# Operands of VectorE in the bring stage of a graph network kernel: SBUF against PSUM

## Chip, cores, metric

One NeuronCore of a Trainium2 chip runs the whole program. The metric is the time of one execution on the device in microseconds (us), median over the runs shown.

## What is computed

Two graph layers over 6250 nodes and 206250 edges (100000 random pairs in both directions and a loop for each node, sorted by destination), each after a layer norm with ReLU and each added to its input:

```
h = max(layernorm(x), 0)
x = x + edge_layer(h)        # per edge: silu(silu([h[src], h[dst], attr, weight/5] @ ew1 + eb1) @ ew2 + eb2)
                             # summed over the edges of a row, then a node MLP, residual
h = max(layernorm(x), 0)
x = x + gat(h)               # two attention layers: 4 heads x 32 with ReLU, then 1 head x 64
```

The edge layer sums by source node, while the edges arrive sorted by destination. So the kernel first brings each edge's part of the hidden layer to its place in an order by source. That is the bring stage, the one that the change is in.

## The kernel before

Edges are cut into chunks of 128 that belong to one tile of 128 destination nodes; four chunks (U = 4) are a group, and the bring stage has 415 groups (SUPER). Each engine runs its own program. `edge_pipeline` writes out the first 8 groups, runs the rest in a loop of 8 groups a round and then the tail; a step of an engine handles a group some steps behind the newest. All order between engines is by counting semaphores that the code waits on; on one engine the order is that of the code.

In the bring stage, for a group:
- SP loads four records of 128 edges (L471) and two columns of places (L473), ScalarE's queue the other two columns (L756).
- VectorE (`bring`, L1309 to L1346) works out the slots: small instructions on 128x4 at L1324, L1327, L1328, L1329, L1337, L1341 and L1343, and one long one at L1334, which compares the row of lane numbers 0..127 (`lanes`) with each edge's lane and so writes a one-hot matrix of 128x512 in bf16. L1341 writes into the buffer `z_out` and waits first (L1339) until the puts of the group eight earlier, which used that buffer, have landed.
- TensorE turns the one-hots and the records (L950, L952), two steps later it multiplies (L935, L938) into banks 2 and 3 of PSUM. It uses banks 0 to 5 in this stage. ScalarE copies out of PSUM (L745, L746, L738).
- GpSimd (`put`, L633 to L642) waits for ScalarE's copy and for VectorE's slots and issues four indirect DMAs at L640, called puts here: each writes 128 rows of 132 numbers to the places in `z_s`, in DRAM, that a column of slots in SBUF names.

Where an edge goes in the order by source is worked out by `rank` (L1231 to L1245), once for each of 49 tiles and each of four parts of the edges (310, 434, 434 and 434 columns). It is five VectorE instructions, each of which waits for the one before: L1237 compares the keys with the tile number into `found`; L1239 is a running sum over `found` (the scan's second operand is a zero, broadcast) into `counted`; L1241 saves its last column; L1243 multiplies the compare with the running sum; L1245 adds that to the places. Part 0 is ranked ahead of the stage (L1251). Parts 1 to 3 are ranked inside it: groups 8 to 151 each carry one `rank` step behind their own instructions (L1344), and at three cuts one more step and the conversion L1249 follow (`next_part`). Then the remaining 263 groups have none.

Behind it come the edge stage (`edge_mlp`), which sums into banks 6 and 7, the node stage and the two attention layers, in which GpSimd gathers rows with an indirect DMA at L690 and VectorE reduces PSUM (L1490, L1486), multiplies (L1576) and adds into sums (L1588 with SBUF operands, L1593 with one operand in PSUM).

All PSUM is one tensor `ps_all`; `ps[n]` is its bank n, 512 fp32 columns wide.

Of the kernel before, what the change touches and what calls it, by code (L numbers as in the profile page):

```python
# [15 lines left out]
ALU = mybir.AluOpType  # L16
# [3 lines left out]
P = 128  # L20
# [7 lines left out]
U = 4  # L28
# [9 lines left out]
PARTS = (310, 434, 434, 434)  # L38
# [106 lines left out]
def part_cols(k):  # L145

    return slice(PART_AT[k], PART_AT[k] + PARTS[k])
# [27 lines left out]
def gnn_kernel(nc, x, ids_in, src_in, dst_next, rec_in, ew1, eb1, ew2, eb2, nw1, nb1, nw2, nb2,  # L175
               W1, a_src1, a_dst1, b1, W2, a_src2, a_dst2, b2, out):
    ctx = ExitStack()
    with ctx:
        def sb(name, shape, dt=F32):
            return ctx.enter_context(nc.sbuf_tensor(name, shape, dt))[tuple(slice(None) for _ in shape)]  # L180

        def sem(name):
            return ctx.enter_context(nc.semaphore(name))
# [28 lines left out]
        lanes = sb("lanes", [P, P])  # L212
# [4 lines left out]
        signs_at = sb("signs_at", [P, NB + 1])  # L217

        picks = [sb(f"pick{n}", [CODE + 3 * h, h, P], BF16) for n, (h, _) in enumerate(LAYERS)]
        lower = sb("lower", [P, P])  # L220
        ones = sb("ones", [P, P])
        ones_b = sb("ones_b", [P, P], BF16)
        zero = sb("zero", [P, 1])
# [52 lines left out]
        def carve(start, shape, dt=F32):  # L276
            words = 1
            for n in shape:
                words *= n
            words = words if dt != BF16 else words // 2  # L280
            v = arena[:, start:start + words]
            assert start + words <= ARENA, (start, shape)
            if dt != F32:
                v = v.bitcast(dt)
            names = " ".join("abcd"[:len(shape)])
            kw = {"abcd"[n]: shape[n] for n in range(len(shape))}
            return v.rearrange(f"p ({names}) -> p {names}", **kw), start + words
# [23 lines left out]
        src_hit, src_scan = (acc[:, 2 * COLS + k * max(PARTS):2 * COLS + (k + 1) * max(PARTS)] for k in range(2))  # L311
# [6 lines left out]
        dst_hot, at = carve(at, [4, U, P], BF16)  # L318
# [49 lines left out]
        ps = [ps_all[:, 512 * n:512 * (n + 1)] for n in range(8)]  # L368
# [3 lines left out]
        def S(name):  # L372
            if name not in s:
                s[name] = sem(name)
            return s[name]

        block = ctx.enter_context(nc.Block())

        class Rounds:
# [5 lines left out]
            def load(self, i):  # L385
                _, self.values = nc.values_load_multi_w_load_instructions(
                    self.table[0:1, bass.ds(i - self.back, self.count)], engines=(self.engine,), min_val=0, max_val=self.top,
                    skip_runtime_bounds_check_because="counts of comparisons, and starts that a minimum bounds")

            def of(self, g):  # L390
                if g.i is None:
                    return self.eng.value_load(self.table[0:1, bass.ds(g.at, 1)], min_val=0, max_val=self.top)
                return self.values[g.off + self.back]

        def four(engine, table, g, top):
            _, values = nc.values_load_multi_w_load_instructions(
                table[0:1, bass.ds(g.at * U, U)], engines=(engine,), min_val=0, max_val=top,
                skip_runtime_bounds_check_because="counts of comparisons, and starts that a minimum bounds")
            return values

        @block.sync
        def _(sp):
            sp.dma_start(xs, x.rearrange("(t p) f -> p t f", p=P)).then_inc(S("x_in"), 16)

            for to, ends, name in ((dst_i, ids_in[1:2, :].rearrange("a n -> (a n)"), "dst_in"), (next_i, dst_next, "next_in"), (src_i, src_in, "src_in")):
                for k in range(len(PARTS)):
                    sp.dma_start(to[:, part_cols(k)], edges_of(ends, k).rearrange("(p j) -> p j", p=P)).then_inc(S(name), 16)
            sp.wait_ge(S("weights_clear"), 2)
            loads = [
                (w_src, ew1[0:F_IN, :]), (w_dst, ew1[F_IN:2 * F_IN, :]),  # L410
# [713 lines left out]
        def _(dve):  # L1124
            link = Chain(dve, S("dve_step"))
# [105 lines left out]
            def rank(k, tile, ran):  # L1231

                small = S("rank_step")
                no, come = lanes[:, bass.ds(tile, 1)], carry[:, bass.ds(tile, 1)]
                keys, places = key[:, part_cols(k)], place[:, part_cols(k)]
                found, counted = src_hit[:, 0:PARTS[k]], src_scan[:, 0:PARTS[k]]
                dve.tensor_scalar(found, keys, no, None, ALU.is_equal).then_inc(small, 1)  # L1237
                dve.wait_ge(small, ran + 1)
                dve.tensor_tensor_scan(counted, found, zero.broadcast_to([P, PARTS[k]]), come, ALU.add, ALU.add).then_inc(small, 1)  # L1239
                dve.wait_ge(small, ran + 2)  # L1240
                dve.tensor_scalar(come, src_scan[:, PARTS[k] - 1:PARTS[k]], 1.0, None, ALU.mult).then_inc(small, 1)  # L1241
                dve.wait_ge(small, ran + 3)
                dve.scalar_tensor_tensor(counted, keys, no, counted, ALU.is_equal, ALU.mult).then_inc(small, 1)  # L1243
                dve.wait_ge(small, ran + 4)
                dve.tensor_tensor(places, places, counted, ALU.add).then_inc(small, 1)  # L1245
# [5 lines left out]
            with dve.Fori(0, NT) as b:  # L1251
                rank(0, b, b * RANK_STEPS)
# [49 lines left out]
            link(dve.tensor_copy(b_part[:, 2, :], b_rest))  # L1302
            dve.sem_inc(S("b_part_ready"), 1)


            dve.wait_ge(S("ordered"), 1)
            dve.sem_inc(S("arena_free"), 1)

            def bring(of):  # L1309
                g = of(0)  # L1310
                if g is None:
                    return
                r = g.slot(4)
                small = S("slot_step")

                def after(k):
                    dve.wait_ge(small, g.back(1).done(SLOT_STEPS) + k)

                dve.wait_ge(S(f"rec_in{r}"), g.uses(4, 16 * U))
                src_col = xr[:, r, :, REC - 2:REC - 1].bitcast(I32).rearrange("p u a -> p (u a)")  # L1320
                dst_col = xr[:, r, :, REC - 1:REC].bitcast(I32).rearrange("p u a -> p (u a)")
                if g.back(1).exists():
                    after(0)
                dve.scalar_tensor_tensor(beyond, lane_node[:, bass.ds(g.at * U, U)], lane_rest, dst_col, ALU.add, ALU.is_le  # L1324
                                         ).then_inc(small, 1)
                dve.wait_ge(S(f"slot_in{r}"), g.uses(4, 16 * U))
                dve.tensor_tensor(to_spare, spare[:, g.slot(SLOTS) * U:(g.slot(SLOTS) + 1) * U], slot_in[:, r], ALU.subtract).then_inc(small, 1)  # L1327
                dve.tensor_scalar(lane_i[:, r], src_col, P - 1, None, ALU.bitwise_and).then_inc(small, 1)  # L1328
                dve.scalar_tensor_tensor(dst_lane[:, r], dst_col, lane_col, lane_node[:, bass.ds(g.at * U, U)], ALU.add, ALU.subtract  # L1329
                                         ).then_inc(small, 1)  # L1330
                if g.back(4).exists():
                    dve.wait_ge(S("x_transposed"), g.back(4).done())
                after(4)
                dve.tensor_tensor(dst_hot[:, r], lanes.unsqueeze(1).broadcast_to([P, U, P]),  # L1334
                                  dst_lane[:, r].unsqueeze(2).broadcast_to([P, U, P]), ALU.is_equal).then_inc(S("dst_hot_ready"), 1)
                after(2)
                dve.tensor_tensor(to_spare, to_spare, beyond, ALU.mult).then_inc(small, 1)  # L1337
                if g.back(SLOTS).exists():
                    dve.wait_ge(S(f"z_put{g.slot(SLOTS)}"), g.back(SLOTS).uses(SLOTS, 16 * U))  # L1339
                after(3)  # L1340
                dve.tensor_copy(z_out[:, g.slot(SLOTS), :, F_HID], lane_i[:, r]).then_inc(small, 1)  # L1341
                after(5)
                dve.tensor_tensor(slot[:, g.slot(SLOTS)], to_spare, slot_in[:, r], ALU.add).then_inc(small, 1)  # L1343
                if 0 < ranking[0] < len(PARTS) and g.i is not None:  # L1344
                    first = SLOTS + (ranking[0] - 1) * PART_ROUNDS * SLOTS
                    rank(ranking[0], g.at - first, g.at * RANK_STEPS + (RANK_STEPS * (NT * ranking[0] - first)))  # L1346
# [3 lines left out]
            def next_part():  # L1350
                k = ranking[0]
                if k > 0:
                    rank(k, NT - 1, RANK_STEPS * (NT * (k + 1) - 1))
                    ranked(k)
                ranking[0] += 1
# [303 lines left out]
```

## Time and profile before

| | |
|---|---|
| time of 3 runs | 9367.48, 9372.87 and 9378.12 us, median 9372.87 us |
| profiled execution | 9370.1 us, span of its trace 9368.2 us |
| busy, share of the span | TensorE 77%, GpSimd 68%, VectorE 65%, ScalarE 52% |
| stages, us from the start | set-up and ranking of part 0 to 343; bring stage 343 to 2617; edge stage to about 4360; attention layers from about 4521 and 7000 to the end |
| costliest group | L690, 3616 gathers, 3471.1 us busy |
| second | L640, 1660 puts, 1755.0 us busy, mean 1057 ns |

A busy share is an average over stages that have different limits, so none of these shares says what binds a stage. For that one reads the chain of work that ended last, the busy time by stretch and the order of time within a group. Each time below is from one profiled execution, in us from the start of the span unless marked ns; L640 is line 640 of the kernel.

### The profile page before, as it was taken

How to read it: one execution, taken by the hardware profiler on the slowest of the kernel's cores; microseconds unless marked ns; L12 is line 12 of the kernel's file. 1: busy time of each engine (PE TensorE's matmuls, PEld its weight loads, DVE VectorE, ACT ScalarE, POOL GpSimd, SP SyncE). 2: the span in 40 equal slices, each digit the busy share in tenths (PEclk: the TensorE clock that was granted, in tenths of full speed). 3: DMA queues.
4: the chain of work that ended last, by engine and by line, in shares of the span. 5: the costliest groups of instructions: out<-in, count | busy, mean ns of one | idle time of the engine just before them, and what ended most of it. 6: DMA issues, size and time to landing. Idle time of an engine off the chain costs nothing.

```text
span 9368.2 us, 235997 instructions
## 1 busy us (share of the span) xinstructions
PE 7249.4 (77%) x52596; PEld 5744.2 (61%) x52823; DVE 6071.2 (65%) x27239; ACT 4885.8 (52%) x11854; POOL 6324.9 (68%) x7563
## 2 busy tenths in 40 slices
PE   2466666666689999998699999999966777777776
PEld 2355555555578888887366666666645555555554
DVE  7777732222233343343799999999976777777776
ACT  4122233333334444443467667777736777777775
POOL 0377777777766666663577777777737777777775
PEclk9988888888899999999555555555555555555555
DMA  4122222222222222221222222222241111111114
GB/s 142 43 54 55 54 59 60 59 61 60 60 75 70 70 72 70 71 71 33 54 55 54 55 54 55 54 55 54 55 33 29 28 28 28 28 28 28 28 28 27
DMA packets 990523, 491.42 MB, mean 52 GB/s; under 512 B 830665, under 2 KB 841468, under 8 KB 990140
## 3 DMA queue, kind: packets, MB, share of 16 engines
q0 software_dynamic: 168832, 302.29, 14.8%
q1 hardware_dynamic: 701756, 169.41, 9.8%
q10 hardware_dynamic: 119840, 18.68, 1.2%
q8 instruction: 31, 0.51, 0.0%
q14 instruction: 64, 0.52, 0.0%
HBM read 356.46 MB, written 151.48 MB: 54 GB/s over the span
## 4 chain that ended last, share of the span: by engine, by line
PE 26%; issue 23%; POOL 23%; DVE 17%; DMA 6%; DVEq 2%; ACT 1%; POOLq 1%; SPq 0%; ACTq 0%
POOL z_s L640 18%; DMA arena<-table,arena 5%; POOL arena L690 5%; PE ps_all L965 5%; PE ps_all L975 4%; PE ps_all L992 4%; PE ps_all L1100 3%; PE ps_all L989 3%; DVE shift L1531 2%; DVE arena L1535 2%; DVE arena L1490 2%; PE ps_all L1076 1%; DVE arena L1576 1%; PE ps_all L1001 1%; PE ps_all L977 1%
## 5 line engine op out<-in xcount | busy, mean ns | idle before, releaser
L690 POOL DMA_INDIRECT arena<-table,arena x3616 | 3471.1, 960 | 1500.5 <-issue 984.6
L640 POOL DMA_INDIRECT z_s<-arena x1660 | 1755.0, 1057 | 853.1 <-issue 504.5
L1100 PE MATMUL ps_all<-arena 128*128 128x132 f32 (+1 forms) x7232 | 1809.1, 429 | 1.8 <-DVE acc L1593 1.8
L1100 PEld LDWEIGHTS ps_all<-arena 128*128 128x128 f32 x7232 | 1606.4, 325 | 2.6 <-issue 2.6
L829 ACT ACTIVATE arena<-lanes_b,arena 128x128 bf16<-128x128 bf16 x3616 | 1147.1, 387 | 415.6 <-DVE arena L1464 407.1
L1490 DVE TENSOR_REDUCE arena<-ps_all 128x2 f32<-128x1024 f32 x904 | 1098.2, 1215 | 18.3 <-PE ps_all L1117 18.3
L1117 PE MATMUL ps_all<-arena,pick 28*128 28x512 bf16 (+1 forms) x2260 | 1081.7, 597 | 0.5 <-DVE arena L1490 0.5
L1076 PE MATMUL ps_all<-ident_b,arena 128*128 128x128 bf16 x3616 | 541.0, 303 | 645.1 <-DMA arena<-table,arena 434.0
L745 ACT ACTIVATE arena<-ps_all 18x512 f32<-18x512 f32 x415 | 243.2, 586 | 1381.0 <-PE ps_all L952 1367.2
L1386 DVE TENSOR_TENSOR arena<-lanes,arena 128x512 f32<-128x512 f32 x452 | 322.8, 714 | 973.8 <-PE ps_all L965 973.8
L853 ACT ACTIVATE arena<-ps_all 28x512 bf16<-28x512 bf16 (+1 forms) x904 | 522.6, 578 | 717.2 <-PE ps_all L1076 717.2
L950 PE MATMUL ps_all<-ident_b,arena 128*128 128x128 bf16 x1660 | 188.1, 245 | 822.7 <-DVE arena L1334 821.4
L1076 PEld LDWEIGHTS ps_all<-ident_b,arena 128*128 128x128 bf16 x3616 | 356.3, 136 | 761.3 <-DVE arena L1477 393.9
L1341 DVE CAST arena<-arena 128x4 f32<-128x4 int32 x415 | 72.9, 176 | 1041.3 <-DMA z_s<-arena 1041.2
L1072 PEld LDWEIGHTS ps_all<-ident_b,arena 128*128 128x128 bf16 x3616 | 303.4, 127 | 654.7 <-issue 647.9
L950 PEld LDWEIGHTS ps_all<-ident_b,arena 128*128 128x128 bf16 x1660 | 108.4, 106 | 903.4 <-DVE arena L1334 755.8
L1072 PE MATMUL ps_all<-ident_b,arena 128*128 128x128 bf16 x3616 | 536.9, 302 | 102.6 <-ACT arena L836 102.6
L935 PE MATMUL ps_all<-w_edge,arena 128*128 128x128 f32 x3320 | 604.4, 341 | 10.3 <-issue 9.3
L935 PEld LDWEIGHTS ps_all<-w_edge,arena 128*128 128x128 f32 x3320 | 544.5, 248 | 67.1 <-issue 44.3
L836 ACT ACTIVATE arena<-arena 128x512 bf16<-128x512 bf16 x904 | 568.9, 629 | 30.9 <-ACT arena L829 0.4
L1088 PE MATMUL ps_all<-arena 128*128 128x8 bf16 (+1 forms) x10848 | 447.3, 169 | 162.7 <-DVE arena L1567 156.1
L1088 PEld LDWEIGHTS ps_all<-arena 128*128 128x128 bf16 x10848 | 427.9, 109 | 215.3 <-DVE arena L1567 181.2
(260 smaller groups left out, 16454.3 us busy)
## 6 DMA issues: line engine op xcount, KB each, us to landing
arena<-z_s SPq DMA_DIRECT2D x452, 264.0 KB, 2.7
arena<-table,arena POOLq DMA_INDIRECT x3616
arena<-rec_d SPq DMA_DIRECT2D x1660, 10.0 KB
z_s<-arena POOLq DMA_INDIRECT x1660
rec_d<-in_rec ACTq DMA_DIRECT2D x1, 16160.0 KB, 58.4
arena<-ids_d SPq DMA_DIRECT2D x904, 4.0 KB
arena<-pos_d ACTq DMA_DIRECT2D x830, 0.5 KB
arena<-pos_d SPq DMA_DIRECT2D x830, 0.5 KB
```

The source lines that it names most:

```text
L640: pool.indirect_dma_start(z_s, bass.IndirectOffsetOnAxis(ap=slot[:, g.slot(SLOTS), u:u + 1], axis=0), z_out[:, g.slot(SLOTS), u, :], None) ...
L690: pool.indirect_dma_start(g_rows[:, r, u * step + CODE_WORDS:(u + 1) * step], None, tables[n], bass.IndirectOffsetOnAxis(ap=ids[:, r, 0, u ...
L829: act.activation(lane_gap[:, g.slot(2), u, :], lanes_b, ACT.Square, bias=neg_lane[:, g.slot(4), u:u + 1]).then_inc(S("lane_gap_ready"), 1)
L836: act.activation(a_hot[:, g.slot(SLOTS)], lane_gap[:, g.slot(2)], ACT.Relu, scale=-1.0, bias=1.0).then_inc(S("a_hot_ready"), 1)
L853: act.activation(turned[0:CODE + 3 * heads, g.slot(SLOTS), 1, :], bank[0:CODE + 3 * heads, GE:2 * GE], ACT.Copy).then_inc(S("turned_copied ...
L935: pe.matmul(ps[2 + r][:, u * P:(u + 1) * P], x_t[:, g.slot(4), u * P:(u + 1) * P], w_edge, start=(u == 0), stop=False, skip_group_check=True)
L1072: pe.transpose(bank[:, u * P:(u + 1) * P], a_hot[:, r, u, :], ident_b)
L1076: mm = pe.transpose(bank[:, GE + u * P:GE + (u + 1) * P], g_rows[:, r, u * step:u * step + P // 2].bitcast(BF16), ident_b)
L1088: mm = pe.matmul(ps[5][:, u * 2 * heads:(u + 1) * 2 * heads], turned[:, g.slot(SLOTS), 0, u * P:(u + 1) * P], lk[:, part, :], start=(part ...
L1100: mm = pe.matmul(ps[6][:, 0:out_w], a_hot_f[:, g.slot(4), u, :], g_msg[:, g.slot(4), u * out_w:(u + 1) * out_w], start=(u == 0), stop=(u = ...
L1117: mm = pe.matmul(bank, picks[n][:, h, :], turned[0:CODE + 3 * heads, g.slot(SLOTS), 1, :], start=True, stop=True)
L1490: dve.tensor_reduce(part_max[:, g.slot(4), 2 * pair:2 * pair + 2], ps_all[:, pair * 1024:(pair + 1) * 1024].rearrange("p (h e) -> p h e", ...
```

## The change

Three names are added, all in PSUM: `counted_ps` is bank 6, `zero_ps` one column and `lanes_ps` 128 columns of bank 7. Ahead of the stage VectorE sets `zero_ps` to zero and copies `lanes` into `lanes_ps`. In `rank` for parts 1 to 3 the running sum is written to and read from bank 6 and the zero is read from bank 7; part 0 keeps SBUF. L1334 reads the lane row from bank 7. No instruction is removed, and no wait on another engine is added or taken away.

```diff
+        counted_ps, zero_ps, lanes_ps = ps[6], ps[7][:, P:P + 1], ps[7][:, 0:P]
...
-                found, counted = src_hit[:, 0:PARTS[k]], src_scan[:, 0:PARTS[k]]
+                found = src_hit[:, 0:PARTS[k]]
+                counted, nought = (src_scan[:, 0:PARTS[k]], zero) if k == 0 else (counted_ps[:, 0:PARTS[k]], zero_ps)
                 dve.tensor_scalar(found, keys, no, None, ALU.is_equal).then_inc(small, 1)
                 dve.wait_ge(small, ran + 1)
-                dve.tensor_tensor_scan(counted, found, zero.broadcast_to([P, PARTS[k]]), come, ALU.add, ALU.add).then_inc(small, 1)
+                dve.tensor_tensor_scan(counted, found, nought.broadcast_to([P, PARTS[k]]), come, ALU.add, ALU.add).then_inc(small, 1)
                 dve.wait_ge(small, ran + 2)
-                dve.tensor_scalar(come, src_scan[:, PARTS[k] - 1:PARTS[k]], 1.0, None, ALU.mult).then_inc(small, 1)
+                dve.tensor_scalar(come, counted[:, PARTS[k] - 1:PARTS[k]], 1.0, None, ALU.mult).then_inc(small, 1)
                 dve.wait_ge(small, ran + 3)
                 dve.scalar_tensor_tensor(counted, keys, no, counted, ALU.is_equal, ALU.mult).then_inc(small, 1)
                 dve.wait_ge(small, ran + 4)
...
+            link(dve.memset(zero_ps, 0.0))
+            link(dve.tensor_copy(lanes_ps, lanes))
+
...
-                dve.tensor_tensor(dst_hot[:, r], lanes.unsqueeze(1).broadcast_to([P, U, P]),
+                dve.tensor_tensor(dst_hot[:, r], lanes_ps.unsqueeze(1).broadcast_to([P, U, P]),
                                   dst_lane[:, r].unsqueeze(2).broadcast_to([P, U, P]), ALU.is_equal).then_inc(S("dst_hot_ready"), 1)
```

## Rows read from the trace of the kernel before

**Rows 1.** Page, part 4, chain that ended last: share of the span by line.
```profile
POOL z_s L640 18%; DMA arena<-table,arena 5%; POOL arena L690 5%; PE ps_all L965 5%; PE ps_all L975 4%; PE ps_all L992 4%; PE ps_all L1100 3%; PE ps_all L989 3%; DVE shift L1531 2%; DVE arena L1535 2%; DVE arena L1490 2%; PE ps_all L1076 1%; DVE arena L1576 1%; PE ps_all L1001 1%; PE ps_all L977 1%
```

**Rows 2.** The same chain from 400 to 1190 us, share of this stretch by line.
```profile
by line: POOL z_s L640 77.0%; issue 21.4%; POOLq L637 0.5%; POOLq L636 0.4%; POOLq L638 0.3%; POOLq L118 0.2%; ACTq L756 0.1%; ACT arena L738 0.1%; ACTq L735 0.0%; ACTq L737 0.0%
```

**Rows 3.** Stretches: length, busy us (xcount) by engine, granted clock, DMA share, GB/s.
```profile
356.20:1195.90 839.70, 512.56 (x3564) 451.79 (x3562) 653.48 (x1918) 247.12 (x447) 663.05 (x580) 0.84 0.27 55
1195.90:2617.40 1421.50, 894.45 (x6328) 790.38 (x6328) 415.44 (x2110) 437.75 (x791) 1091.91 (x1081) 0.85 0.28 60
```

**Rows 4.** Line 640: duration ns min/median/max, first and last start us.
```profile
L640 POOL DMA_INDIRECT z_s<-arena x1660: 954/958/1588, 356.3 to 2616.4; - x185
```

**Rows 5.** Waits, 356.2 to 1195.9 us: who for whom, us in total, times, longest.
```profile
POOL z_s L640 <- issue: 175.7, 576, 0.3
DVE arena L1341 <- DMA z_s<-arena: 134.1, 124, 1.6
```

**Rows 6.** Order of time, VectorE, 700 to 706 us: start, duration, instruction.
```profile
700.47 1.12 DVE L1239 TENSOR_TENSOR_SCAN acc<-acc,carry,zero 128x434 f32<-128x434 f32 x1
...
702.52 0.61 DVE L1245 TENSOR_TENSOR acc<-acc 128x434 f32<-128x434 f32 x1
...
703.59 0.69 DVE L1334 TENSOR_TENSOR arena<-lanes,arena 128x512 bf16<-128x512 f32 x1
...
705.40 0.17 DVE L1341 CAST arena<-arena 128x4 f32<-128x4 int32 x1 [1.05 <-DMA z_s<-arena]
...
705.66 0.45 DVE L1237 TENSOR_SCALAR acc<-acc,lanes 128x434 f32<-128x434 f32 x1
```

**Rows 7.** Order of time, GpSimd, 701 to 706 us.
```profile
701.05 1.31 POOL L640 DMA_INDIRECT z_s<-arena  x1 [0.30 <-issue]
702.67 1.30 POOL L640 DMA_INDIRECT z_s<-arena  x1 [0.30 <-issue]
704.27 0.96 POOL L640 DMA_INDIRECT z_s<-arena  x1 [0.31 <-issue]
705.53 0.96 POOL L640 DMA_INDIRECT z_s<-arena  x1 [0.30 <-issue]
```

**Rows 8.** Order of time in the stretch without ranking, two engines.
```profile
1515.97 0.69 DVE L1334 TENSOR_TENSOR arena<-lanes,arena 128x512 bf16<-128x512 f32 x1
1516.17 1.32 POOL L640 DMA_INDIRECT z_s<-arena  x1 [0.31 <-issue]
```

**Rows 9.** Order of time in the first attention layer, two places.
```profile
4998.95 1.22 DVE L1490 TENSOR_REDUCE arena<-ps_all 128x2 f32<-128x1024 f32 x1
4999.52 0.96 POOL L690 DMA_INDIRECT arena<-table,arena  x1 [0.30 <-issue]
...
4596.88 0.28 DVE L1593 TENSOR_TENSOR acc<-acc,ps_all 128x132 f32 x1
4596.99 0.95 POOL L690 DMA_INDIRECT arena<-table,arena  x1 [0.30 <-PE ps_all L1076]
```

**Rows 10.** Order of time at 2579.8 us, a memset over several puts.
```profile
2579.85 5.45 DVE L1365 MEMSET acc<- 128x6468 f32 x1 [1.30 <-issue]
2581.01 0.95 POOL L640 DMA_INDIRECT z_s<-arena  x1 [0.30 <-issue]
2582.27 0.96 POOL L640 DMA_INDIRECT z_s<-arena  x1 [0.30 <-issue]
```

**Rows 11.** Order of time at 927 us.
```profile
927.29 0.45 DVE L1237 TENSOR_SCALAR acc<-acc,lanes 128x434 f32<-128x434 f32 x1
927.54 1.03 POOL L640 DMA_INDIRECT z_s<-arena  x1 [0.30 <-issue]
```

**Rows 12.** Groups by line and shape, VectorE: busy us, mean ns, idle before.
```profile
L1588 DVE TENSOR_TENSOR acc<-acc,arena 128x132 f32 x452 | 129.1, 286 | 9.8 <-issue 8.1 <-ACT arena L820 1.0 <-DVE acc L1593 0.5
L1593 DVE TENSOR_TENSOR acc<-acc,ps_all 128x132 f32 x452 | 128.1, 283 | 6.4 <-PE ps_all L1100 6.4
L1593 DVE TENSOR_TENSOR acc<-acc,ps_all 128x65 f32 x452 | 100.7, 223 | 241.9 <-PE ps_all L1100 241.9
L1243 DVE SCALAR_TENSOR_TENSOR acc<-acc,lanes 128x434 f32<-128x434 f32 x147 | 98.6, 671 | 5.2
```

**Rows 13.** Line 690: duration ns min/median/max, first and last start us.
```profile
L690 POOL DMA_INDIRECT arena<-table,arena x3616: 949/955/1467, 4521.5 to 9308.7; - x191
```

## Prediction

> **What bounds the kernel now.** I read the chain that ended last first: the one line with the largest share of it is the put of the bring stage, GpSimd's indirect DMA at L640, with 18% of the span [rows 1]. That chain cut to 400 to 1190 us is this line for 77% and GpSimd's own issue time for 21% [rows 2]; nothing of VectorE, TensorE or ScalarE stands in it with more than 0.1%. So only what makes a put longer, or the gap between two puts, is worth anything there, and the stage is one row of 1660 puts.
>
> Next the busy time by stretch [rows 3]. The stage has two stretches: with a ranking step of parts 1 to 3 in each group (356.2 to 1195.9 us, 580 puts, 145 groups) and without (1195.9 to 2617.4 us, 1081 puts). In the first a put takes 663.05/580 = 1.143 us, in the second 1091.91/1081 = 1.010 us. The gap is the same in both: (839.70 - 663.05)/580 = 0.305 us and (1421.50 - 1091.91)/1081 = 0.305 us. Both are above the median put, 0.958 us [rows 4], so some puts are stretched and most aren't. A group of four costs 5.79 us with ranking and 5.26 us without; unstretched it would be 4 x (0.957 + 0.305) = 5.05 us.
>
> Who stretches them shows in the order of time [rows 6, 7]. The scan L1239 runs from 700.47 to 701.59; a put that starts at 701.05, inside it, takes 1.31 us. The add L1245 runs from 702.52 to 703.13; the put that starts at 702.67 takes 1.30 us. Puts that start at 704.27 and 705.53 start in neither and take 0.96 us. Each stretched one ends some 0.8 us after the VectorE instruction does, so the put waits early in its life until that one has finished reading. In the other stretch the one-hot compare L1334 does the same: it starts at 1515.97, the put at 1516.17 takes 1.32 us [rows 8]. All three read two tensors in SBUF.
>
> **What the change does to each of them.** The scan's zero and its output, the multiply's (L1243) and the add's second input, and the lane row of L1334 go to PSUM. After it each of the four long instructions has one SBUF tensor left. The trace has instructions with at most one: while the reduce L1490, PSUM in, runs from 4998.95 to 5000.17, the put-like gather that starts at 4999.52 takes 0.96 us; while L1593 (one input in PSUM, one in SBUF) runs from 4596.88, a gather that starts 0.11 us into it takes 0.95 us [rows 9]. A memset that only writes SBUF covers whole puts of 0.95 and 0.96 us [rows 10], so it isn't the write side either. The reduce is strong: it is 1.22 us long, runs 904 times, and the median of all 3616 gathers is still 955 ns [rows 13]. L1593 is weak, being only 0.28 us long.
>
> *Gain, ranking stretch:* 663.05 - 580 x 0.957 = 108.0 us. *Gain, other stretch:* 1091.91 - 1081 x 0.957 = 57.4 us. Together 165.4 us, all on the chain.
>
> *L1237 stays as it is* (one SBUF tensor in, SBUF out, 0.45 us for 434 elements where the add L1245 needs 0.61, so a faster form) [rows 6]. It does hold a put that starts in its middle: it starts at 927.29, the put at 927.54 takes 1.03 us [rows 11]. It doesn't touch a put that started before it: it lies wholly inside the put of 705.53, which takes 0.96 us [rows 6, 7]. Will it fall on a start after the change? VectorE's group begins when the fourth put of the group eight earlier has landed: L1341 starts at 705.40, 1.43 us after that put ended at 703.97. L1237 follows 0.26 us later, 1.69 us after that end; puts start at 0.30, 1.56, 2.83 and 4.09 us after it. That phase hangs on the landing, not on the stretched puts, so it stays: L1237 starts 0.13 us after a put did, as now. I leave 4 us for jitter (some 20 hits of 0.2 us).
>
> The Trainium skill has a rule that speaks against this. Its page "SBUF — State Buffer", section "Who interferes with whom" and the box on SWDGE, says that a VectorE instruction in a two-port mode takes the port pair for its whole length and that GpSimd then can't write descriptors. By it L1237 would cost up to 0.45 us in each of 144 groups, 65 us in sum, and the time would come to some 9277 us. The put of 705.53, which has all of L1237 inside it and isn't longer, disagrees; the one of 927.54 agrees.
>
> *What PSUM operands cost VectorE.* Reading: the add with one input in PSUM, L1593, takes 283 ns at 132 elements, its twin with both in SBUF, L1588, 286 ns [rows 12]. So 0 for a read. Writing PSUM from VectorE isn't in the trace. Its lower bound is the same 0 (slightly below is possible, no reason excludes it), its upper bound, if the multiply L1243 reads and writes the same bank at half pace, is one more pass of its 434 elements: L1245 spends 0.61 us on 434 [rows 6], so at most 0.6, and since part of that is fixed I call it 0.45 us a group: L1593 at 132 elements takes 283 ns and at 65 elements 223 ns [rows 12], 0.9 ns an element, 0.39 us for 434. I take 0.05 us for the scan and the multiply together, since the reads are nearest.
>
> Does VectorE then still fit? In the ranking stretch it idles 134.1 us at L1341 for landings [rows 5], 134.1/145 = 0.92 us a group, so its own chain is 5.79 - 0.92 = 4.87 us. The puts' new period is 5.05 us. So 0.18 us a group is left, and **VectorE is what is late next**. Even past that there is a reserve: it runs eight groups ahead of the puts, TensorE and ScalarE need about three of them, so some four groups (20 us) can be eaten before a put waits. TensorE is busy 512.56 of 839.70 us [rows 3], 3.5 us a group, under 5.05.
>
> The skill prices PSUM otherwise: "VectorE: DVE Perf Modes", section on the TRN2 errata, gives a fixed 120 cycles from PSUM against 58 from SBUF. An estimate from it is 65 ns on each of five instructions, 0.32 us a group; VectorE would then be the bound at 5.19 us, 0.14 x 145 = 20 us in sum, which the reserve just covers. L1593 against L1588 disagrees.
>
> *Added:* a one-element memset and a copy of 128x128 into PSUM ahead of the stage, chained. The add of 132 elements (286 ns, rows 12) bounds the copy; with the waits 0.5 us in sum, on the path, once. No DMA, no queue and no wait between engines is added; GpSimd, SP and ScalarE keep their streams. Where the stage ends earlier, everything behind it only shifts: no later instruction changes.
>
> **Sum.** 165.4 - 4 - 0.5 = 161 us. The profiled span 9368.2 us becomes 9207, the profiled execution's 9370.1 us becomes 9209, and from the median 9372.87 us, 2.8 us above it, 9212 us.
>
> **Rivals.**
> *A, L1334 goes on holding puts.* In the add-like rows that have a PSUM operand it is the second one; in L1334 the lane row is the first and the SBUF tensor the second. If the second operand comes by the shared way whatever the first is, the 57.4 us stay lost. In the ranking stretch L1334 would start 5.37 us after the landing put's end, modulo 5.05 that is 0.32, against a put's start at 0.30: a coin's throw, 0 to 72 us, I take 20. Gain 165 - 57 - 20 - 5 = 83 us: 9290 us.
> *B, VectorE becomes the bound.* With 0.45 us more in L1243 its chain is 5.32 us: 0.27 x 145 - 20 = 19 us lost of the gain, 9231 us.
> *C, nothing changes.* The put is held not by the second SBUF tensor but by any long streaming read of SBUF; for it speaks L1237's hold, against it L1593 and nothing else with an SBUF tensor. All four still stream one. 9373 us.
> *D, slower.* VectorE's accesses to PSUM, the scan's and the multiply's above all, run at a fraction of the pace. The time turns when the ranking group exceeds (57.4 + 20)/145 = 0.53 us more than today's 5.79, that is a chain of 6.32 us, 1.45 us more than now. Two more passes in each of L1239 and L1243 (4 x 0.45 = 1.8 us) give 6.67 us: 0.88 x 145 - 20 - 57 = 51 us slower, 9424 us. Against it: L1593 reads PSUM as fast as L1588 reads SBUF.
>
> **How the numbers follow.** As forecast 0.78 (own range 9202 to 9235, the upper end with L1237 falling in the way or a write price of 0.2 us); A 0.10, B 0.05, C 0.04, D 0.03. 0.2% is 19 us, about what a measurement of this kernel can tell from no change. Forecast, A and B are faster by more: 0.93; C 0.04; D 0.03. The range must hold 8 in 10: low 9200, since the end of all stretching at no cost is 9372.87 - 165.4 = 9207, less 7 us of scatter; high 9280, which takes in B, takes in L1237 holding a put by 0.3 us in each of 145 groups (44 us, 9256), and reaches towards A. The forecast and B are 0.83.
>
> **What would show it.** Right: in both stretches the mean put is 0.96 to 0.97 us, the stage ends near 2456 us, gaps stay 0.305 us; VectorE's wait at L1341 in the ranking stretch falls from 0.92 to some 0.15 us a group; L1243 keeps 0.67 us [rows 12], L1245 0.61 and the scan 1.12. A shows as puts of 1.3 us in the second stretch alone; B as a chain that leaves L640 for VectorE before 1200 us; C as 1.14 and 1.01 us kept; D as a scan or multiply well over a microsecond longer. Later stages that differ by more than some microseconds, the granted clock in them included, would mean that I left something out.

## Result: the bring stage gave what was expected, the first attention layer took more

| | before | changed |
|---|---|---|
| median of 5 runs each | 9369.36 us | 9415.76 us |
| ratio to before | | 1.0048, 95% interval 1.0033 to 1.0062 |
| profiled execution, span | 9370.1, 9368.2 us | 9420.4, 9418.6 us |
| bring stage, first put to last | 356.3 to 2616.4 us | 356.0 to 2456.4 us |
| first attention layer, first to last reduce | 4534.7 to 6929.0 us | 4375.5 to 6975.5 us |

The change makes the kernel slower by 0.5%, where 1.7% faster was forecast. In the changed kernel the same code stands some lines lower: L640 is L643, L1237 L1241, L1239 L1243, L1334 L1341, L1341 L1348, L1490 L1497, L1516 L1523, L690 L693; in the kernels of the experiments a line or two off that.

Busy time by stretch of the changed kernel, the two stretches of the bring stage and the two attention layers, columns as in [rows 3] (length, then busy us of TensorE, its weight loads, VectorE, ScalarE and GpSimd, granted clock, DMA share, GB/s):

```profile
355.90:1091.40 735.50, 492.84 (x3571) 433.57 (x3569) 656.53 (x1917) 247.63 (x447) 558.80 (x580) 0.86 0.30 63
1091.40:2457.40 1366.00, 907.73 (x6328) 803.06 (x6328) 412.59 (x2111) 437.77 (x791) 1037.10 (x1080) 0.83 0.29 62
4375.40:6975.50 2600.10, 2222.05 (x14386) 1461.24 (x14384) 2298.96 (x10791) 1659.80 (x4495) 1750.23 (x1798) 0.53 0.27 51
7082.30:9383.80 2301.50, 1692.74 (x13016) 1331.37 (x13015) 1596.43 (x10338) 1610.00 (x4493) 1722.61 (x1798) 0.50 0.22 28
```

The attention layers in the kernel before, same view:

```profile
4534.70:6929.10 2394.40, 2214.06 (x14386) 1458.46 (x14384) 2287.47 (x10792) 1658.61 (x4495) 1732.69 (x1798) 0.54 0.29 54
7035.90:9333.50 2297.60, 1692.67 (x13015) 1331.32 (x13014) 1591.76 (x10338) 1609.34 (x4493) 1718.71 (x1798) 0.50 0.22 28
```

Against [rows 3], the stretch with ranking went from 839.7 to 735.5 us and the one without from 1421.5 to 1366.0 us: 160 us won. The first attention layer went from 2394.4 to 2600.1 us: 206 us lost, with the engines nearly as busy as before (VectorE 2287 and 2299 us, GpSimd 1733 and 1750 us) and TensorE's granted clock at 0.54 and 0.53. So nearly all of the 206 us is idle time. The second layer took 4 us more. 160 - 206 - 4 = -50 us is the difference of the spans. The gap between two puts stayed at 0.305 us, (735.5 - 558.80)/580 and (1366.0 - 1037.10)/1080.

Puts, as in [rows 4] (min/median/max ns, first and last start):

```profile
L643 POOL DMA_INDIRECT z_s<-arena x1660: 955/962/1156, 356.0 to 2456.4; - x185
```

What VectorE waited for in the first attention layer, before and then changed (us in total, times, longest):

```profile
DVE arena L1516 <- issue: 75.9, 61, 1.5
DVE arena L1490 <- PE ps_all L1117: 18.3, 13, 10.9
```

```profile
DVE arena L1523 <- issue: 270.7, 60, 8.6
DVE arena L1497 <- PE ps_all L1120: 16.3, 10, 10.9
```

L1523 (L1516 before) is the first instruction of VectorE's loop, which handles eight groups a round, 54 rounds. Ahead of it VectorE waits for no engine and no DMA that the profile shows; the time is "issue", in the mean 1.2 us a wait before and 4.5 us now. That is 195 of the 206 us. The order of time at such a place of the changed kernel:

```profile
4581.36 0.17 DVE L1482 TENSOR_SCALAR arena<-arena 128x32 bf16<-128x32 int32 x1
4581.44 0.17 DVE L1484 TENSOR_SCALAR arena<-arena 128x32 bf16<-128x32 int32 x1
4586.64 0.16 DVE L1523 TENSOR_SCALAR arena<-dst_parts 128x12 bf16 x1 [5.03 <-issue]
```

One line of the page's part 3 moved with it, the queue that brings instructions (packets, MB, share of the engines): before, then changed.

```profile
q14 instruction: 64, 0.52, 0.0%
```

```profile
q14 instruction: 329, 2.70, 0.1%
```

265 packets more of 8.2 KB each are five a round in 53 rounds. The trace also dates each packet. Between the first and the last branch of this loop on VectorE, 53 rounds, one packet falls in the kernel before and 266 in the changed one, five in each round and one more in one of them; in the second layer's loop there is none in either.

### The profile page after: what moved, and what is told of

It reads as the page before. It is cut to its first block, busy times and chain, and to the rows that moved or that the text cites. A ratio compares the mean times of both kernels' runs of the same rounds, so it can differ in the third digit from the quotient of the medians.

```text
span 9418.6 us, 236225 instructions
## 1 busy us (share of the span) xinstructions
PE 7263.0 (77%) x52822; PEld 5741.1 (61%) x52823; DVE 6087.3 (65%) x27241; ACT 4887.8 (52%) x11854; POOL 6189.3 (66%) x7563
## 4 chain that ended last, share of the span: by engine, by line
PE 26%; issue 25%; DVE 19%; POOL 18%; DMA 7%; DVEq 3%; ACT 1%; POOLq 0%; ACTq 0%; SPq 0%
POOL z_s L643 12%; POOL arena L693 5%; DMA arena<-table,arena 5%; PE ps_all L968 5%; PE ps_all L978 4%; PE ps_all L995 4%; PE ps_all L1103 3%; PE ps_all L992 3%; DVE arena L1542 2%; DVE shift L1538 2%; DVE arena L1497 2%; PE ps_all L1079 1%; DMA z_s<-arena 1%; DVE arena L1583 1%; PE ps_all L1004 1%
## 5 line engine op out<-in xcount | busy, mean ns | idle before, releaser
L693 POOL DMA_INDIRECT arena<-table,arena x3616 | 3492.4, 966 | 1688.6 <-issue 957.9
L643 POOL DMA_INDIRECT z_s<-arena x1660 | 1595.9, 961 | 852.2 <-issue 475.9
L1497 DVE TENSOR_REDUCE arena<-ps_all 128x2 f32<-128x1024 f32 x904 | 1097.3, 1214 | 16.3 <-PE ps_all L1120 16.3
L1348 DVE CAST arena<-arena 128x4 f32<-128x4 int32 x415 | 75.0, 181 | 879.1 <-DMA z_s<-arena 878.0
```

The source lines that it names most:

```text
L643: pool.indirect_dma_start(z_s, bass.IndirectOffsetOnAxis(ap=slot[:, g.slot(SLOTS), u:u + 1], axis=0), z_out[:, g.slot(SLOTS), u, :], None) ...
L693: pool.indirect_dma_start(g_rows[:, r, u * step + CODE_WORDS:(u + 1) * step], None, tables[n], bass.IndirectOffsetOnAxis(ap=ids[:, r, 0, u ...
L1497: dve.tensor_reduce(part_max[:, g.slot(4), 2 * pair:2 * pair + 2], ps_all[:, pair * 1024:(pair + 1) * 1024].rearrange("p (h e) -> p h e", ...
```

## Theories

**Code.** The change adds two VectorE instructions ahead of the bring stage. They move every later loop of VectorE by two places in its code. The loop of the first layer is the longest, some 357 instructions in the built program. If code is held in blocks and only a few blocks stay, a loop that touches one block more is fetched anew in every round. **Rival: what the change does.** PSUM operands, or an attention layer that starts 160 us earlier (buffers, TensorE's clock), slow the layer. The clock row above already speaks against the clock, the runs below decide.

All kernels of e1 to e8 ran on chips where the kernel before takes 9370 to 9380 us (median of the runs beside them).

## e1 and e2: the two instructions without their use, and the use without the shift

e1 is the kernel before with this alone, nothing reads the two tiles:

```diff
+        counted_ps, zero_ps, lanes_ps = ps[6], ps[7][:, P:P + 1], ps[7][:, 0:P]
...
+            link(dve.memset(zero_ps, 0.0))
+            link(dve.tensor_copy(lanes_ps, lanes))
```

> The kernel before with the two added VectorE instructions (the memset of one PSUM column and the copy of the lane row into PSUM) and nothing that reads them. All of rank and L1334 stay in SBUF. Code theory: the two instructions move VectorE's loop of the first attention layer by two places, and the loop then has to be fetched again in each round; expected are about 265 more packets of the instruction queue (329 in place of 64), some 3.6 us of idle time at the head of each of 54 rounds, the first attention layer at 2600 us in place of 2395 and a total of about 9370 + 206 = 9576 us. Rival, PSUM operands or an earlier end of the bring stage (TensorE's clock, buffers) slow the attention layer: nothing of this is in the kernel, so 9370 us.

Measured: 9581.86 us, ratio 1.0220 (1.0203 to 1.0237), and

```profile
q14 instruction: 329, 2.70, 0.1%
```

```profile
DVE arena L1522 <- issue: 273.3, 62, 8.7
```

Two instructions of well under a microsecond cost 211 us. Neither the reads of PSUM nor the earlier start are in this kernel, so the rival falls.

e2 is the changed kernel with seven instructions fewer in the set-up:

```diff
-            for half in range(2):
-                for bit in range(LANE_BITS + 1):
-                    at = half * (CODE // 2) + bit
-                    link(dve.memset(bit_masks[:, at:at + 1], 1 << bit if bit < LANE_BITS else -P))
+            for bit in range(LANE_BITS + 1):
+                link(dve.memset(bit_masks[:, bit:bit + 1], 1 << bit if bit < LANE_BITS else -P))
+            link(dve.tensor_copy(bit_masks[:, CODE // 2:], bit_masks[:, 0:CODE // 2]))
```

> The changed kernel with seven VectorE instructions fewer in the set-up: the second eight of sixteen one-column memsets of the bit masks become one copy. Code theory: the loops lie five places earlier than in the kernel before, the instruction queue is back at about 64 packets, the first attention layer at 2395 us, the bring stage still ends near 2456 us, total about 9415 - 206 = 9209 us. Rival (PSUM operands, clock): the attention layer stays at 2600 us, total 9414 us.

Measured: 9206.48 us against 9370.5 us, ratio 0.9822 (0.9805 to 0.9838).

```profile
q14 instruction: 64, 0.52, 0.0%
```

```profile
354.90:1089.10 734.20, 493.72 (x3563) 434.58 (x3562) 656.91 (x1917) 246.53 (x445) 557.29 (x580) 0.86 0.30 63
1089.10:2452.30 1363.20, 906.10 (x6328) 800.81 (x6328) 411.35 (x2111) 437.80 (x791) 1034.04 (x1080) 0.83 0.29 62
```

```profile
L1496 DVE TENSOR_REDUCE arena<-ps_all x904: 1205/1215/1225, 4369.8 to 6762.5; 128x2 f32<-128x1024 f32 x181
```

The layer takes 2392.7 us again and the bring stage keeps its 164 us. This version beats both kernels.

## e8: the shorter set-up by itself

The kernel before with e2's shorter set-up.

> The kernel before with only the set-up shortened by seven instructions, as in e2. It says what of e2's gain is the shortening itself: the code theory expects nothing beyond the instructions' own 1 us, 9369 us with 64 packets. If the shorter set-up were a gain of its own (a better place of the loops, say) it would be clearly under 9360 us.

Measured: 9369.03 us against 9380.32 us, ratio 0.9989 (0.9979 to 0.9999), 64 packets. At most 0.2% of e2's 1.8% is the set-up.

## e3, e4, e7: how many places matter

e7 adds one memset at the start of VectorE's program of the kernel before; e3 and e4 add 104 and 164 there to the changed kernel:

```diff
             link(dve.memset(zero, 0.0))
+            for _ in range(104):
+                link(dve.memset(zero, 0.0))
```

> The kernel before with one more one-column memset at the start of VectorE's program, so that its loops lie one place later, not two. Code theory: it is either still well placed (64 packets, 9370 us) or already badly placed (329 packets, 9575 us), nothing between; which one it is says whether the loop's last place before was the block's last or the last but one. Rival, a cost that grows with the number of added instructions: some 9470 us.

> The changed kernel with 104 more one-column memsets at the very start of VectorE's program, some 12 us of work of which about 10 lie under the load of x. Code theory, what counts is where the loop lies against the blocks that are fetched and not how much code stands ahead of it: if a block holds 128 instructions (or 256) the loop has fallen on a good place again, about 64 packets and a first attention layer of 2395 us, total 9212 to 9225 us. Rival, more code ahead makes it worse or leaves it: 2600 us, 9415 to 9430 us.

> The changed kernel with 164 more one-column memsets at the start, up to 20 us of work, half of it under the load of x. With blocks of 128 instructions the loop of the first attention layer lies badly again, and that of the second layer as well: over 500 more packets, both layers 150 to 206 us longer, total 9560 to 9640 us. With blocks of 256 instructions both lie well: 64 packets, 9220 us.

Measured: e7 9586.28 us (ratio 1.0219, 1.0202 to 1.0236) with 330 packets, so the loop sat at its last good place before, and one instruction costs as much as two. e3 9214.6 us (0.9831, 0.9815 to 0.9847) with 65 packets: with 104 instructions more than the changed kernel it is as fast as e2, but for 8 us. e4 9384.36 us (1.0014, 1.0004 to 1.0024), with

```profile
q14 instruction: 595, 4.87, 0.2%
```

595 - 65 = 530 is twice 265, and by their times 265 of the packets fall in the first layer's loop and 264 in the second's: both are fetched anew. But only one pays. The first to last reduce of the two layers of e4:

```profile
L1499 DVE TENSOR_REDUCE arena<-ps_all x904: 1206/1215/1225, 4382.8 to 6939.8; 128x2 f32<-128x1024 f32 x181
...
L1495 DVE TENSOR_REDUCE arena<-ps_all x452: 677/691/693, 7050.8 to 9350.9; 128x1 f32<-128x512 f32 x151
```

The first takes 2557 us, 163 more than before; the second 2300 us, 2.5 more. In the first the wait at the loop's head is 210.5 us here, where it was 270.7 in the changed kernel, for as many packets: which bad place it is changes the price too, and why was not worked out. VectorE does stand idle at the head of its loop in the second too, in e4 and then in the kernel before:

```profile
DVE arena L1525 <- issue: 225.4, 69, 4.7
DVE acc L1602 <- PE ps_all L1103: 176.4, 325, 0.6
DVE arena L1565 <- PE ps_all L1091: 159.8, 244, 2.5
DVE arena L1495 <- PE ps_all L1120: 79.5, 324, 3.1
```

```profile
DVE acc L1593 <- PE ps_all L1100: 238.9, 390, 0.6
DVE arena L1556 <- PE ps_all L1088: 209.6, 375, 2.5
DVE arena L1486 <- PE ps_all L1117: 104.9, 390, 10.2
DVE arena L1516 <- PE ps_all L1088: 80.0, 54, 1.6
...
DVE arena L1516 <- issue: 5.6, 16, 1.0
```

220 us more of idle time there cost 2.5 us, because VectorE isn't what bounds that layer: its waits for TensorE shrink in exchange, from 633 us in the four rows of the kernel before to 416 us in the three of e4. My expectation for e4, 150 to 206 us in each layer and 9560 us or more in all, was wrong in the second layer and so in the total.

## e9, e10, e11, e12: the other edge, and two chips on which every kernel is slower

Let a block hold B instructions and a loop of 357 be kept while it touches k blocks. Then kB - 356 places in B are good and the bad run between is 356 - (k - 1)B long (with a loop of 356 it is one place shorter). The changed kernel with 97 and with 99 more memsets puts the loop 99 and 101 places behind where it was in the kernel before.

> The changed kernel with 97 more one-column memsets at the start. The first attention loop is some 357 instructions of VectorE and the kernel before was at the last good place. If code is fetched in blocks of 128 and a loop of this length is kept as long as it touches three of them, 28 or 29 starting places in 128 are good, and the next good one after the changed kernel's is reached with 98 or 99 more instructions. So 97 is still bad: about 329 packets or more, the first attention layer some 150 to 206 us longer, total 9370 to 9430 us. Rival, blocks of another size or a slow drift with the amount of code: no edge here, the same count of packets as with 99.

> The same with 99 more instructions, two more than the run beside it. With blocks of 128 this is the first or second good place: about 65 packets, the first attention layer as before, total 9212 to 9225 us. Rival, blocks of another size: no edge, both alike.

The queue's row of e9, then of e10:

```profile
q14 instruction: 595, 4.87, 0.1%
```

```profile
q14 instruction: 65, 0.53, 0.0%
```

The edge is there, between 99 and 101 places; by their times, e9's packets fall in both layers' loops, 266 and 265, and e10's don't. The bad run goes from 1 to 99 or 100: B is 128 with k = 3, or 256 with k = 2. With 256 the place of e4, 166, would be good; it is bad. So blocks hold **128 instructions**, and this loop must lie in three of them; 28 or 29 places in 128 are good. The times came out far from what I wrote: 12737 us and 12609 us, because in these two runs the kernel before itself took 12458 us. Even so e9 takes 129 us more than e10, beside it and with two instructions fewer. I repeated e2's kernel and e9's.

> The kernel of e2 once more, since e9 and e10 ran on a chip on which the kernel before itself took 12458 us. On a chip on which the kernel before takes about 9370 us: 9206 us again, 64 packets. On one like that of e9 and e10: a bring stage of 7.3 us a group with puts of 0.96 us that wait for the loads, so nothing of the 165 us can be won there, and the time is that of the kernel before within 1.5%.

> The kernel of e9 once more (97 more memsets at the start, both attention loops badly placed by e9's 595 packets). On a chip on which the kernel before takes about 9370 us: 595 packets; as in e4, whose packets were as many, the first attention layer some 160 to 210 us longer and the second unchanged, 9370 to 9430 us, although two instructions more (e10) need 65 packets.

Both again ran on a chip where the kernel before is slow, another one: the kernel before 12446.47 us, e11 12596.77 us (ratio 1.0123, 1.0106 to 1.0140), e12 12724.89 us (1.0228, 1.0211 to 1.0245), 65 and 595 packets. e11 is within the 1.5% that I expected for such a chip; neither shows the time on a chip of 9370 us. The bring stage of e11, as one stretch, and what was waited for in it:

```profile
354.50:3411.10 3056.60, 1527.68 (x9891) 1392.13 (x9889) 1080.48 (x4027) 666.39 (x1237) 1590.91 (x1660) 0.73 0.21 43
```

```profile
ACT arena L748 <- remote: 1944.7, 199, 12.6
DVE arena L1330 <- DMA arena<-rec_d: 1150.7, 303, 9.2
POOL z_s L643 <- ACT arena L741: 1089.3, 154, 345.2
```

The puts are 1590.91/1660 = 0.958 us, unheld, but a group takes 7.4 us: VectorE waits for the records and GpSimd for ScalarE (345.2 us of that ahead of the first put), which waits for something that the profile doesn't name. The puts aren't what sets the pace there, so making them shorter can't be expected to pay. One difference is in SP's queue, in the line that loads the records, e11 and then e2 (ns min/median/max):

```profile
L474 SPq MOVE arena<-rec_d x1660: 2/29/1307, 335.8 to 3371.8; - x185
```

```profile
L474 SPq MOVE arena<-rec_d x1660: 29/29/42, 335.8 to 2395.4; - x185
```

A register move that takes 29 to 42 ns on one chip takes up to 1307 ns on the other; the median, 29 ns, is the same, and whether such moves cause the slowness isn't shown. Each chip was met at one time only, so chip and time can't be told apart either. **Open:** why e2's kernel isn't as fast as the kernel before there but 1.2% slower; no profile of the kernel before on such a chip exists. The code theory holds on both: with the same change in it, badly placed loops and 97 memsets cost 128 us there (e12 against e11).

## e5 and e6: the two halves of the change

e5 is e2 with `lanes` back in L1334, e6 is e2 with rank back in SBUF.

> The kernel of e2 (seven set-up instructions fewer, the change in it) with L1334 reading the lane row from SBUF again; the running sum and its zero stay in PSUM. If the hold comes from the second SBUF tensor alone: in the second stretch puts stay at 1.01 us and a group at 5.26 us (57 us not won). In the ranking stretch the scan and the add no longer hold; L1334 now starts within 0.02 us of a put's start, so a group costs between 5.06 and 5.5 us, I expect 5.15. Total 9206 + 57 + 14 = about 9277 us, between 9263 and 9325.

> The kernel of e2 with rank back in SBUF; only L1334 reads PSUM. Second stretch: puts at 0.958 us, a group at 5.05 us, 57 us won. Ranking stretch: the scan and the add hold one put each in every group as before, 5.79 us. Total about 9370 - 57 = 9313 us. If the holds add up otherwise (L1334 also held puts in the ranking stretch), up to 10 us less.

Measured: e5 9269.24 us, e6 9307.12 us, both against 9380.32 us (ratios 0.9881, 0.9865 to 0.9898, and 0.9925, 0.9909 to 0.9942). The two stretches of e5, then of e6:

```profile
354.70:1094.80 740.10, 498.45 (x3564) 437.89 (x3562) 660.08 (x1917) 247.08 (x447) 563.16 (x580) 0.85 0.30 62
1094.80:2512.10 1417.30, 896.68 (x6328) 793.48 (x6328) 415.13 (x2110) 437.76 (x791) 1088.01 (x1080) 0.84 0.28 60
```

```profile
354.30:1189.50 835.20, 502.70 (x3564) 442.04 (x3562) 653.24 (x1918) 246.84 (x446) 658.35 (x580) 0.85 0.27 55
1189.50:2553.30 1363.80, 904.88 (x6328) 799.57 (x6328) 410.71 (x2110) 437.73 (x791) 1034.60 (x1080) 0.83 0.29 62
```

With L1334 on SBUF the second stretch keeps puts of 1088.01/1080 = 1.007 us; with it on PSUM they are 0.958 us. With the scan and the add on SBUF the first keeps 658.35/580 = 1.135 us; on PSUM 0.971 us. Each half gives its own stretch. Against [rows 3] L1334 alone (e6) wins 4 us in the first and 58 us in the second, rank alone (e5) 100 us in the first and 4 us in the second. In the first stretch of e5, where the prediction saw 0 to 72 us for L1334, it cost 6 us (740.1 against 734.2): in the three groups from 800 to 812 us it starts 0.15 to 0.28 us after a put did, and those puts take 0.96 us.

The same shows put by put. In the kernel before 147 puts start inside the add, with a median of 1301 ns, and 142 inside the scan, median 1321 ns; in the changed kernel 71 start inside the add and 91 inside the scan, and none takes more than 976 ns. Of the 274 that start inside the compare none takes more than 1022 ns, before the longest of 289 took 1479 ns. One under the scan and one under the compare in the changed kernel:

```profile
703.62 1.13 DVE L1243 TENSOR_TENSOR_SCAN ps_all<-acc,carry,ps_all 128x434 f32<-128x434 f32 x1
704.05 0.96 POOL L643 DMA_INDIRECT z_s<-arena  x1 [0.30 <-issue]
...
1706.07 0.69 DVE L1341 TENSOR_TENSOR arena<-ps_all,arena 128x512 bf16<-128x512 f32 x1
1706.27 0.96 POOL L643 DMA_INDIRECT z_s<-arena  x1 [0.31 <-issue]
```

## Why the prediction was wrong

- **The sum for the bring stage** was right. Forecast 165.4 - 4 = 161 us, measured 160 us (and 164 us in e2). Puts: forecast 0.96 to 0.97 us, measured 558.80/580 = 0.963 and 1037.10/1080 = 0.960. End of the stage: forecast 2456, measured 2457.
- **Who holds a put**: e5 and e6 show it, each on the stretch it was forecast for. Rival A (L1334 goes on holding) is out: 0.958 us in e6. C (any long read of SBUF holds) is out: the scan and the compare still read one SBUF tensor, and the puts that start inside them take 0.96 us.
- **PSUM's price** was taken as 0.05 us; the scan takes 1126 ns for 1122, the multiply 675 for 671 [rows 12], the add 607 for 611. So B and D are out, and so are, for these instructions, the 65 ns more that the prediction estimated from the Trainium skill ("VectorE: DVE Perf Modes", section on the TRN2 errata). VectorE's idle time for landings fell to 24.1 us over 145 groups, 0.17 us, forecast 0.15:

```profile
DVE arena L1348 <- DMA z_s<-arena: 24.1, 59, 1.4
```

```profile
L1243 DVE TENSOR_TENSOR_SCAN ps_all<-acc,carry,ps_all 128x434 f32<-128x434 f32 x146 | 164.3, 1126 | 18.7 <-DVE acc L1241 1.6
...
L1247 DVE SCALAR_TENSOR_TENSOR ps_all<-acc,lanes,ps_all 128x434 f32<-128x434 f32 x146 | 98.5, 675 | 6.0 <-DVE carry L1245 0.6
L1249 DVE TENSOR_TENSOR acc<-acc,ps_all 128x434 f32<-128x434 f32 x146 | 88.6, 607 | 5.0
L1241 DVE TENSOR_SCALAR acc<-acc,lanes 128x434 f32<-128x434 f32 x146 | 72.7, 498 | 0.0
```

- **L1237** cost as little as forecast: all that is left of stretching in the ranking stretch is 558.80 - 580 x 0.957 = 3.7 us, for the 4 us allowed. The reason given was wrong. Its start, 0.14 us after a put's in the median before, did not stay there but went to 0.46 us, and 22 puts start inside it in place of 5, the longest of them 1148 ns. That so few do is in part luck. The put of 705.53 was also no evidence against the rule that it was set against, since it had started before L1237. L1237 itself takes 498 ns in the mean now, for 451. The traces say when: where it starts 0.4 to 0.7 us after a put did it takes up to 689 ns, elsewhere 447 ns in the median and 508 at most; 60 of 147 start so late, in place of 11. That the put holds it would fit; no run tested it.
- **The step that failed** is "Added": a memset and a copy, "0.5 us in sum, on the path, once", and with it "everything behind it only shifts: no later instruction changes". No later instruction changed, but their places in the code did: VectorE's loop of the first attention layer came to touch a fourth block of code and was fetched again in each round. The term was 211 us (e1), not 0.5. The four rivals were all about what holds puts and what PSUM costs. That D's 9424 us lies near the measured 9416 us is chance: its mechanism, a scan and a multiply slower by 1.8 us together, measured 4 ns each. The warning was in the list of what would make the forecast wrong (later stages that differ), without a mechanism or a price, and the range had none either.

What could have been seen ahead: the page of the kernel before counts the packets of instructions, 64 for the whole program, and of these one falls in the 53 rounds of this loop, so it wasn't fetched again. What it can't show is how close a loop lies to the edge; for that one counts the loop's instructions and has to know the block. Here a loop of 357 has 3 x 128 - 356 = 28 good places in 128 and 100 bad ones, and the kernel before sat at the last of the good ones.

## What to carry to other kernels

An edit that adds or removes even one instruction on an engine moves that engine's later loops in their code, and here one was enough (e7); read the instruction queue's packets of both profiles before you judge the edit, and where they grew, move the loop (a few set-up instructions more or fewer) and measure again. Where GpSimd's indirect DMAs are the chain, a long VectorE instruction that reads two SBUF tensors lengthens each of them that starts inside it (here, under the scan and the add, from 0.96 to 1.3 us in the median, 1.59 us at most); put one of the two in PSUM. Price an idle time by whether its engine is the bound: the same refetch cost 163 us in one layer and 2.5 us in the next.

## What the runs showed of the hardware

- VectorE's code is fetched in blocks of 128 instructions (8.2 KB a packet), and a loop that touches three of them is kept, one that touches four isn't. This is worked out for the loop of some 357 instructions, from the edges at 0/1 and 99/101 places and from e4. Once it isn't kept, each round fetches five packets, 265 in 53 rounds, and waits some 3.3 us more at its head (270.7 us over 60 waits against 75.9 us over 61).
- The Trainium skill, "Runtime: NRT & Kernel Launch", section "Instruction fetch mechanics", gives blocks of 16 KiB, 256 instructions, of which two are held, and calls the cost of crossing one mostly hidden. It also warns that a taken branch to a target outside the two held blocks stalls the engine until the block is fetched. By its block size e4's place would be good: on that these runs disagree (8.2 KB, 128 instructions). On the branch they agree, and they give it a price, 206 us in 53 rounds. The page of the kernel before has a second instruction queue, q8, with 31 packets of 16.5 KB; which engine's code it brings isn't shown.
- These VectorE instructions of 434 fp32 elements read and write PSUM at the pace of SBUF, the same bank in one instruction included: the multiply, whose second input and output are both in bank 6, takes 675 ns for 671.
- A put that starts while VectorE reads two SBUF tensors waits; one that starts while it reads one from SBUF and one from PSUM doesn't, whichever of the two is the first operand (0.96 us under the compare with the PSUM tensor first, and under the scan and the add with it second). A put that started 0.15 to 0.28 us before the compare did isn't held (0.96 us, three groups of e5).
- In the other direction L1237, which reads one SBUF tensor and writes one, takes up to 689 ns for 447 where it starts 0.4 to 0.7 us after a put did. That the put is what holds it isn't tested.
- On two of the chips the same kernel took 12.4 ms in place of 9.4 ms, and there the longest register move of SP's load line took 1307 ns for 42. A gain measured on one chip needn't be there on another: e2's kernel is 1.8% faster than the kernel before on one and 1.2% slower on another.
